# Second layer's node pass taken out of the dense stage and woven into three convolutions of a four-layer graph network

## The reference

```python
h = relu(layernorm(x)); x = x + L0(h)     # L0: gated messages with edge_attr_32, segment sum over dst,
                                           #     update MLP, residual, layernorm with gain and bias
h = relu(layernorm(x)); x = x + L1(h)     # L1, below
h = relu(layernorm(x)); x = x + L2(h)     # L2: x[src] @ W + b, segment mean over dst
h = relu(layernorm(x)); x = x + L3(h)     # L3: three graph convolutions with degree norms, each with a relu

def L1(h):
    e = relu(concatenate([h[src], h[dst]]) @ Wm1 + bm1) @ Wm2 + bm2
    m = segment_sum(e * edge_attr_96, dst, 100000)
    return relu(concatenate([h, m]) @ Wu1 + bu1) @ Wu2 + bu2
```

## Time and profile before

| what | value |
|---|---|
| median of three executions | 6417.43 us (6413.93 to 6429.01) |
| profiled execution, own time | 6405.65 us |
| its span | 6403.8 us |
| busy over the span | PE 66%, PE weight loads 44%, DVE 64%, ACT 53%, POOL 53% |
| mean granted TensorE clock | 0.753 of 2.4 GHz |
| HBM traffic | 97 GB/s on average |
| dense stage / e0 / e1 | 1569 / 820 / 874 us |
| convolutions 0, 1, 2, 3 | 555, 528, 529, 1015 us |

### The profile page before, as it was taken

The page is one execution under the profiler, slowest core; times in us unless marked ns, Lnnn a source line. Parts: engine busy times, 40 slices in busy tenths (PEclk is TensorE's granted clock), DMA queues, the critical chain, the costliest instruction groups (busy, mean ns, idle before and its releaser), DMA issues. The chain is left out here.

```text
span 6403.8 us, 106282 instructions
## 1 busy us (share of the span) xinstructions
PE 4235.2 (66%) x19615; PEld 2819.0 (44%) x19615; DVE 4067.5 (64%) x12933; ACT 3425.7 (53%) x8726; POOL 3406.1 (53%) x3541
## 2 busy tenths in 40 slices
PE   5776888888888899997888865554554554222222
PEld 2224556565555344444555544443444443222221
DVE  5666777777777888887777756665664443222222
ACT  6996888888887899994555532222222221111110
POOL 0004454555453644434444447657775776777777
PEclk9997898989998999998999975555555555555555
DMA  0002444444443434434545445554445997333332
GB/s 16 0 0 83 127 129 124 128 126 125 128 127 120 97 94 94 94 79 108 128 123 128 122 102 136 135 128 91 105 103 86 104 100 92 59 66 66 66 67 59
DMA packets 1064587, 619.13 MB, mean 97 GB/s; under 512 B 843258, under 2 KB 1016582, under 8 KB 1064493
## 3 DMA queue, kind: packets, MB, share of 16 engines
q1 hardware_dynamic: 951532, 469.15, 26.8%
q0 software_dynamic: 112960, 148.99, 16.3%
HBM read 368.52 MB, written 251.78 MB: 97 GB/s over the span
## 5 line engine op out<-in xcount | busy, mean ns | idle before, releaser
L659 POOL DMA_INDIRECT xs<-t,idx x1176 | 1109.8, 944 | 812.3 <-DMA idx<-at 419.0
L1095 PE MATMUL bank<-ident,msg 128*96 128x128 f32 (+1 forms) x1568 | 424.7, 426 | 1033.5 <-ACT msg L914 853.3
L1102 PE MATMUL bank<-w,aggT 96*128 96x96 f32 (+1 forms) x3136 | 771.4, 427 | 429.2 <-DVE aggT L1373 428.6
L1102 PEld LDWEIGHTS bank<-w,aggT 96*128 96x128 f32 (+1 forms) x3136 | 704.7, 330 | 533.0 <-issue 458.7
L914 ACT ACTIVATE msg<-xs,now 128x96 f32<-128x96 f32 x784 | 229.3, 363 | 1293.0 <-DMA xs<-c,idx 846.5
L659 POOL DMA_INDIRECT xs<-c,idx x784 | 750.5, 957 | 310.3 <-issue 232.1
L1095 PEld LDWEIGHTS bank<-ident,msg 128*96 128x96 f32 (+1 forms) x1568 | 288.7, 218 | 1096.1 <-ACT msg L914 735.8
L1373 DVE TENSOR_TENSOR_SCAN aggT<-goes,aggT,bank 96x512 f32<-96x512 f16 (+1 forms) x490 | 621.1, 1268 | 163.3 <-PE bank L1062 88.2
L659 POOL DMA_INDIRECT got<-info_d,idx x392 | 382.3, 975 | 618.4 <-DMA found<-got 514.0
L659 POOL DMA_INDIRECT xd<-in_x_dram,idx x392 | 377.0, 962 | 426.0 <-DVE xn L1443 230.0
L1541 DVE SCALAR_TENSOR_TENSOR y<-bank,now,rows 128x96 f32<-128x96 f32 x392 | 97.2, 311 | 702.3 <-PE bank L1102 702.3
(11 more groups left out here) (213 smaller groups left out, 10297.6 us busy)
## 6 DMA issues: line engine op xcount, KB each, us to landing
t<-xo SPq DMA_DIRECT2D x392, 192.0 KB, 3.2
t<-xn SPq DMA_DIRECT2D x294, 192.0 KB, 2.3
xd<-t SPq DMA_DIRECT2D x294, 192.0 KB, 3.5
goes<-goes_d SPq DMA_DIRECT2D x392, 128.0 KB
xd<-in_x_dram SPq DMA_DIRECT2D x196, 192.0 KB, 2.4
out_dram<-oo SPq DMA_DIRECT2D x196, 192.0 KB
c<-xn SPq DMA_DIRECT2D x196, 192.0 KB
x_src<-xs SPq DMA_DIRECT2D x196, 96.0 KB
```

What stands on the lines that cost most here:

```text
L659: nc.gpsimd.indirect_dma_start(out=into, out_offset=None, in_=table, in_offset=bass.IndirectOffsetOnAxis(ap=indices, axis=0)).then_inc(don ...
L1095: ins = nc.tensor.transpose(bank[g.at(2)][0:m, c * P:(c + 1) * P], msg[:, g.at(2), c, 0:m], ident[:])
L1102: ins = nc.tensor.matmul(tok(bank[2 + g.at(2)], m)[:, c, :], aggT[0:m, g.at(3), c * P:(c + 1) * P], w2[:] if k == 0 else w3[:, k - 1, :], ...
```

## The change

The second layer's node pass leaves the dense stage. A node group of it is now done in two of three steps of the convolutions 0, 1 and 2 (66 node groups a convolution, `woven`): its x1 rows are loaded twice from t1 (once to be normalised, once as residual, so that no buffer is held in between), and only `out` is stored, with relu(b2) already in the bias of `wu2_out`. In the dense stage the root chain serves two kinds.

Convolution 0 used to gather the results of the node pass for sources without an incoming edge from t2. It now gathers them from a table that e1 writes by edge: e1 has the x1 row of each edge's source in hand and computes the node pass on it (`home_z`, `home_act`, `home_u`, `home_x`, `home_store`) for every edge. The tables of row indices (`at`) are computed to match. In e1 `messages` now writes bank 2, which `hid` uses too, so that bank 4 is free; the order of stages on TensorE and ScalarE is changed.

The core of the diff:

```diff
+def woven(eng, k, stages, node_stages):
+
+
+    most = max(stage[1] for stage in stages)
+    last = EG + most if k < 2 else max(EG + most, EG + 10)
+    turns = (EG - 1 - WOVEN_FIRST) // UNROLL - (1 if k == 2 else 0)
+
+    def step(g):
+        for stage, lag in stages:
+            if g.turn is not None or 0 <= g.c - lag < EG:
+                stage(g.shift(-lag))
+        if g.c % 3 < 2 and (g.turn is not None or g.c < EG or k == 2):
+            node = Group(g.turn, k * NODE_STEPS + g.c // 3 * 2 + g.c % 3, NODE_PER)
+            for stage, lag in node_stages:
+                if g.turn is not None or 0 <= node.c - lag < NG:
+                    stage(node.shift(-lag))
+
+    for i in range(WOVEN_FIRST):
+        step(Group(None, i))
+    with eng.Fori(0, turns) as turn:
+        for c in range(UNROLL):
+            step(Group(turn, WOVEN_FIRST + c))
+    for i in range(WOVEN_FIRST + turns * UNROLL, last):
+        step(Group(None, i))
...
+            def node_load(g):
+                need(sp, nd["norm"], g.j - 3)
+                sp.sem_inc(sp_turn, 1)
+                sp.dma_start(node_x[:, g.at(4), :, :], node_view(t1, node_start(g.j) + E_PAD)).then_inc(nd["x_in"][g.at(4)].sem, 16)
+
...
+                sp.sem_inc(sp_turn, 1)
+                sp.dma_start(node_res[:, g.at(4), :, :], node_view(t1, node_start(g.j) + E_PAD))\
+                    .then_inc(nd["x_again"][g.at(4)].sem, 16)
+
...
-                    stages = [(gather_idx(ph, plane), 0), (own_load, 1), (goes_load, 3), (edge_load, 3), (res_load, 4), (edge_store, done)]
+                    stages = [(gather_idx(ph, plane), 0), (own_load, 1), (goes_load, 3), (edge_load, 3), (res_load, 4), (home_store, 6), (edge_store, done)]
...
 
-                plane = (2, 3, 4, 4)[k]
+                plane = (0, 3, 4, 4)[k]
...
-                pipelined(sp, EG, stages)
+                if k < 3:
+                    woven(sp, k, stages, [(node_load, 0), (node_res_load, 3), (node_store, 7)])
+                else:
+                    pipelined(sp, EG, stages)
...
-                    need(pool, ph["norm"] if ph is e0 else ph["norm_s"], g.j - 5)
+                    need(pool, ph["norm"] if ph is e0 else ph["fin_h"], g.j - 5)
...
-                        need(pool, dn["x2_out"][s], ended(NG, 3, s))
-                    if k == 3:
...
-                t = (t2[0:E_PAD + N, :], t2, c1, c2)[k]
+                t = (t2[0:2 * E_PAD, :], t2, c1, c2)[k]
...
+            def node_evac(g):
+                need(act, nd["t1"], g.j + 1)
+                need(act, nd["z1"], g.j - 1)
+                nc.scalar.activation(hsT[0:D, g.at(2), :], bank[4][0:D, :], ACT.Copy).then_inc(nd["r1"].sem, 1)
+
+            def node_relu(g):
+                need(act, nd["z1"], g.j + 1)
+                need(act, nd["u1"], g.j - 1)
+                nc.scalar.activation(v1[0:D, g.at(2), :], bank[5 + 2 * g.at(2)][0:D, :], ACT.Relu, bias=bias[:, 4:5])\
+                    .then_inc(nd["g1"].sem, 1)
 
...
+                def home_act(g):
+                    need(act, ph["zh"], g.j + 1)
+                    need(act, ph["uh"], g.j - 1)
+                    nc.scalar.activation(v1[0:D, g.at(2), :], bank[4][0:D, :], ACT.Relu, bias=bias[:, 4:5])\
+                        .then_inc(ph["gh"].sem, 1)
...
-                    pipelined(act, EG, [(hidden, 2), (update_act, 4), (norms, 0), (evac_s, 0)])
+                    pipelined(act, EG, [(update_act, 4), (hidden, 2), (home_act, 1), (norms, 0), (evac_s, 0)])
...
+                    woven(act, k, [(rows_in, 3 if k < 2 else 0)], [(node_evac, 3), (node_relu, 4), (node_norm, 2)])
+                else:
+                    pipelined(act, EG, [(rows_in, 0)])
...
+            def node_z(g):
+                need(pe, nd["r1"], g.j + 1)
+                need(pe, nd["g1"], g.j - 1)
+                products(bank[5 + 2 * g.at(2)][0:D, :], wu1[:, 0, :], hsT[0:D, g.at(2), :], nd["z1"])
+
+            def node_out(g):
+                need(pe, nd["g1"], g.j + 1)
+                need(pe, nd["x1"], g.j)
                 for c in range(G):
-                    ins = nc.tensor.matmul(tok(bank[5 + 2 * g.at(2)])[:, c, :], v1[:, g.at(2), c * P:(c + 1) * P],
-                                           wu2[:], start=True, stop=True)
...
-                    need(pe, ph["act"], g.j)
+                    need(pe, ph["msg"], g.j)
                     nc.tensor.matmul(bank[2][0:D, :], wm1[:, 0, :], hsT[0:D, g.at(2), :], start=True, stop=False)
                     need(pe, ph["evac"], g.j + 1)
                     nc.tensor.matmul(bank[2][0:D, :], wm1[:, 1, :], hdT[0:D, g.at(6), :], start=False, stop=True)\
...
+                def home_z(g):
+                    need(pe, ph["evac_s"], g.j + 1)
+                    need(pe, ph["fin_h"], g.j)
+                    products(bank[4][0:D, :], wu1[:, 0, :], hsT[0:D, g.at(2), :], ph["zh"])
+
+                def home_u(g):
+                    need(pe, ph["gh"], g.j + 1)
+                    for c in range(G):
+                        ins = nc.tensor.matmul(tok(bank[4])[:, c, :], v1[:, g.at(2), c * P:(c + 1) * P], wu2[:],
+                                               start=True, stop=True)
+                    ins.then_inc(ph["uh"].sem, 1)
...
-                    pipelined(pe, EG, [(hid, 2), (turn_messages, 3), (upd_z, 4), (messages, 2), (upd_u, 4), (tr, 0)])
+                    pipelined(pe, EG, [(upd_z, 4), (hid, 2), (turn_messages, 3), (home_z, 1), (upd_u, 4), (messages, 2),
+                                       (home_u, 1), (tr, 0)])
+                    need(pe, ph["fin_h"], EG)
...
+                stages = [(turn_rows, 3), (apply_w, 4)] if k < 2 else [(turn_rows, 0), (apply_w, 1)]
+                if k < 3:
+                    woven(pe, k, stages, [(node_z, 3), (node_out, 4), (node_turn, 2)])
+                else:
+                    pipelined(pe, EG, stages)
...
+                    b, t, w = g.c // 2 % 2, g.use(2), 2 * G
+                    roots(node_mv[:, b, :, :],
+                          (var[:, 0:w], guess[:, 0:w], (sq[:, 0, 0:w], sq[:, 1, 0:w]), (res[:, 0, 0:w], res[:, 1, 0:w]), root1[:, 0:w],
+                           node_rstd[:, b, :], node_nmr[:, b, :]),
+                          ((nd["my"], g.j + 1), (nd["norm"], g.j - 3)), nd["root"], ROOT * t)
+
+            def node_finish(g):
+                need(dve, nd["x_again"][g.at(4)], landed(g, 4))
+                need(dve, nd["o_out"][g.at(2)], freed(g, 2))
                 dve.sem_inc(dve_turn, 1)
-                nc.vector.tensor_tensor(xo[:, g.at(3), :, :], xn[:, g.at(6), :, :], tok(bank[5 + 2 * g.at(2)]), ALU.add)\
...
-                need(dve, dn["o_out"][g.at(3)], freed(g, 3))
-                dve.sem_inc(dve_turn, 1)
-                need(dve, dn["fin"], g.j + 1)
-                nc.vector.tensor_tensor(oo[:, g.at(3), :, :], xo[:, g.at(3), :, :], wide(relu_b2[:]), ALU.add)\
-                    .then_inc(dn["oo"].sem, 1)
+                need(dve, nd["u1"], g.j + 1)
+                nc.vector.tensor_tensor(oo[:, g.at(2), :, :], node_res[:, g.at(4), :, :], tok(bank[6]), ALU.add)\
+                    .then_inc(nd["x1"].sem, 1)
 
             def dense_state(g):
...
 
             dve.wait_ge(info_out, 16)
-            pipelined(dve, NG, [(times_g(dn), 4), (finish_x, 7), (plus_x, 4), (finish_o, 7), (plus_b, 4), (mom_x, 0),
-                                (mom_y, 2), (mom_z, 4), (roots_of(dn, dense_state), 0, NG + 4)])
...
+            pipelined(dve, NG, [(times_g(dn), 4), (plus_x, 4), (plus_b, 4), (mom_x, 0), (mom_y, 2),
+                                (roots_of(dn, dense_state, kinds=2), 0, NG + 2)])
...
             nc.vector.tensor_copy(norms_of[:, 0, :], found[:, :, 1])
             nc.vector.tensor_copy(at[:, 2, :], found[:, :, 0])
             nc.vector.tensor_scalar(at[:, 4, :], found[:, :, 0], float(E_PAD), None, ALU.min)
             dve.wait_ge(rows_found, 1)
-            nc.vector.tensor_tensor(at[:, 3, :], found[:, :, 0], in_tab[:], ALU.add).then_inc(rows_found, 1)
+            nc.vector.tensor_tensor(out_at[:], out_at[:], in_tab[:], ALU.mult).then_inc(rows_found, 1)
+            dve.wait_ge(rows_found, 2)
+            nc.vector.tensor_tensor(out_at[:], out_at[:], found[:, :, 0], ALU.add).then_inc(rows_found, 1)
+            nc.vector.tensor_scalar(in_tab[:], in_tab[:], -2.0 * E_PAD, 2.0 * E_PAD, ALU.mult, ALU.add).then_inc(rows_found, 1)
+            dve.wait_ge(rows_found, 4)
+            nc.vector.tensor_copy(at[:, 0, :], out_at[:])
+            nc.vector.tensor_tensor(at[:, 3, :], out_at[:], in_tab[:], ALU.add).then_inc(rows_found, 1)
             dve.wait_ge(ends_found, 16)
...
+                def home_x(g):
+                    need(dve, ph["h_out"][g.at(3)], freed(g, 3))
+                    dve.sem_inc(dve_turn, 1)
+                    need(dve, ph["uh"], g.j + 1)
+                    nc.vector.tensor_tensor(oo[:, g.at(3), :, :], xs[:, g.at(6), :, :], tok(bank[4]), ALU.add)\
```

(20 more changed lines are left out.)

175 lines of the change are left out of this document (90 added, 85 removed).

## The result

| | before | after |
|---|---|---|
| median | 6419.96 us (4 runs) | 6821.79 us (4 runs) |
| ratio | | 1.0622, 95% interval 1.0605 to 1.0639 |
| profiled execution, own time | 6405.65 us | 6816.94 us |
| span | 6403.8 us | 6815.1 us |
| mean granted clock | 0.753 | 0.693 |

What follows compares the result with a forecast made beforehand. No engine bounds the whole; each stage has its own round. Dense -369, row indices +3, e1 +45, convolutions +34, +30, +40 sum to -217: 6405.65 to 6189, plus 12 for the median, 6200 us; range 6080 to 6380.

Steps and rivals of the forecast that it cites:

- e1: Second edge layer's stage: home_z adds 0.86 us a group, a steadier clock giving some back; +45 us, between 0 and +150.
- a third of the time low: Dense stage: assumed share of time at TensorE's low clock, giving 5.9 us a round, 1200 us, -369 us.
- 5.3 forecast: Dense stage: a round at the high clock takes 5.3 us.
- 7.5 us: Dense stage: a round at the low clock, a ping-pong between TensorE and ScalarE, takes 7.5 us.
- -485: Dense stage: best end of the forecast's range, the clock never falling, 1084 us.
- Rival B: Dense stage: TensorE's clock falls and stays at 1.2 GHz, 1515 us there, 6515 us in all; chance 9%.
- Rival A: Convolutions 0 to 2: no spare time beside POOL, 6.3 to 6.4 us a group, +320 us, 6416 us; chance 7%.
- +40: Convolution 2: moved loads and stores with the drain add 40 us, between 0 and +115.
- a share of 0.93 leaves 0.07: Convolution 2: DMA busy 0.93 of the stage leaves 0.07 for the moved loads and stores.
- may well get shorter: Convolution 2: the gathers' packets may get shorter with fewer in flight; 5.6 us a group taken.
- +34 and +30: Convolutions 0 and 1: woven node work adds 34 and 30 us, between +5 and +95 each.
- 5.7 and 5.5 us: Convolutions 0 and 1: time a group, VectorE's bound with part of TensorE's some 6.3 us at the low clock.

Runs made afterwards that it cites:

- fill8: Changed kernel with eight extra constant transposes on TensorE in each dense round, four and four: 6269.16 us, ratio to before 0.9791.
- fill12: Changed kernel with twelve extra constant transposes on TensorE in each dense round, six and six: 6269.24 us, ratio to before 0.9773.
- fill4: Changed kernel with four extra constant transposes on TensorE in each dense round, two and two: 6821.03 us, ratio to before 1.0633.
- lag2: Changed kernel with SyncE issuing convolution 2's segment flags and norms three steps earlier: 6671.79 us, ratio to before 1.0403.
- convboth: fill12 and lag2 together, plus extra TensorE transposes in convolutions 0 to 2 and no node-pass moments or root chain on VectorE there: 5988.44 us, ratio 0.9346.
- nohome: fill12 and lag2 together, without e1's home_z, home_u and home_act, VectorE adding source rows to themselves: 5997.96 us, ratio to before 0.9362.
- bfill: Kernel before the change with eight extra transposes in each dense round, four and four: 6300.32 us, ratio to before 0.9835.
- kick: Changed kernel with twelve extra transposes a round in the first dozen or so dense rounds only: 6787.5 us.

## Why the prediction was wrong, point by point

**Dense stage: the share of the low clock.** The step that failed reads "I take a third of the time low, a little more than the 24% of before because the gaps grow", with, two sentences ahead of it, "No row shows this pattern". It was all of the time. fill8 and fill12 show that the high-clock round was sized right (5.3 forecast, 5.31 measured) and that filling TensorE's idle gaps decides whether it comes about; fill4 and the changed kernel show the other level. The price of the low round was also too small: 7.5 us, where the timeline has 8.21. Of the 0.7 us, 0.40 is z1: the 1.74 us came from a product that began at 1587.01, as the clock fell: its 1.70 us stand between the 1.10 of the high level and the 2.02 of the low one in the timeline after, where it is 2.14 us from z1 to the Gelu. A row that straddles a change of the clock is a row of neither level. With 8.2 us the switch between -485 and +38 hangs on one quantity that no row of before fixed; a forecast should then have put its chances on the two ends, not on a mean between them. Rival B was the right mechanism ("TensorE's clock falls and stays at 1.2 GHz"). It had 9%, and "Against: at the low clock it would work 5.9 of 7.5 us, 79%" was no argument: fill4 worked 91% there and stayed low. Even B's 6515 us was 307 short, 92 of them in the dense stage (1515 us against 1607); the ring of convolution 2 is in none of the rivals. Rival A's 1932 us for the three convolutions, near the measured 1941, are luck: it spreads them evenly, some 640 each, where they were 604, 601 and 736.

The Trainium skill (TensorE: Matmul & The Clock Gate, "A second HAM failure mode: psum-queue depth-cycling") has small idles between groups of matmuls make the clock swing. The direction was right, and I gave it too little. Here the dense stage shows one steady 0.50 rather than a swing, though no wait of TensorE in the round above is longer than 0.93 us; convolutions 0 and 1, at 0.66, do swing (the clock falls 30 times in each).

**Convolution 2: a ring through SyncE, not seen.** The prediction costed the moved DMAs as bytes (+40, where lag2 leaves 52 standing) and never followed SyncE's queue. The code had what was needed. SyncE's instructions run in order; its waits for `node_norm` and `node_finish` let it run at most three steps ahead of ScalarE and VectorE; and it issues the loads for VectorE at lags 4 and 5. In convolutions 0 and 1 VectorE uses them at lags 4 and 5 of its own, so SyncE need only keep level with it and has three steps of slack. In convolution 2 VectorE uses them at lags 1 and 2, so SyncE has to be three steps ahead, which is just as far as its waits allow: no slack. lag2 takes back 157 us by two numbers alone.

In the same working, "so a share of 0.93 leaves 0.07" did not hold: in lag2 the share is 0.93 as before, with 158 GB/s instead of 99. The other guess there, that the gathers' packets "may well get shorter", is borne out: 13.28 MB took 77.4% of the engines for 350 us, and in lag2 13.67 MB took 51.6% for 400 us (5150:5550), 20 and 15 us per MB.

**Convolutions 0 and 1: +54 and +69 against +34 and +30.** The mechanism was named (VectorE at 5.2 and 4.9 us, TensorE at 5.8 if the clock stays low) and the size was not: the prediction took VectorE's bound "with part of" the other, where convboth shows two limits of one round that have to go together. The +34 and +30 also don't follow from the 5.7 and 5.5 us as written: 98 groups of them are 4 and 11 us over the 555 and 528 of the earlier trace rows, and the ramps that make up the rest are not given.

**e1: +42 against +45, for another reason.** The working had home_z in the loop at +0.86 us a group and the steadier clock giving half of it back. The clock did go from 0.93 to 0.98. But nohome puts the home products and their ReLU at +125 and everything else of the change in e1 (order of the stages, `messages` on bank 2, `hid`'s wait, clock) at -83. bfill, whose e1 is that of before, reads 867 at 0.94. Two errors of opposite sign met, so the number was luck. What in the order gave the 83 us was not isolated.

**e0 and convolution 3** did not move. That the forecast's own test sentence named 1150 to 1280 us with a mean clock of 0.75 to 0.9 made the dense miss visible in one row.

## What to carry to other kernels

Taking work off a loop in which TensorE and ScalarE answer each other can drop TensorE's clock for the whole stage; then ask for the loop at both levels, treat them as two outcomes, and if it falls, fill TensorE's waits with products of a constant (here eight a round, 548 us). Where plain DMAs of two pipelines share one in-order queue, work out for each stage how many steps the queue may fall behind before a wait in it stands ahead of a load that the same ring needs; that depends on the consumer's lag, and so differs between stages with the same code. A stage forecast that is right as a number says nothing on its terms.

## What the runs showed of the hardware that was not expected

- Four more transposes a round than fill4 took the dense stage from 1607 to 1059 us, and four more than that to 1056. No count between four and eight was tried.
- In kick the granted clock was 1.00 from 526 to about 590 us and 0.50 for the 1497 us behind it, with TensorE busy for 1212 of them; in the kernel before it rose again each time that it had fallen.
- In convolution 2 the same DMA share, 0.93, went with 99 GB/s in the kernel before and with 158 GB/s in lag2. The share of busy time didn't tell how much more the engines could move.
